# GpSimd's one-operation passes as product and addition, and VectorE's tap and copy exchanged, in the feed-forward stage of a gated cross-attention block

## The chip, the cores and the metric

The kernel runs on one core of a Trainium2 chip. Its time is the device time in microseconds (us) of one execution. The engines work side by side, each through its own instructions in order, and wait for one another by semaphores: TensorE (PE in the rows, its weight loads PEld), VectorE (DVE), ScalarE (ACT), GpSimd (POOL) and SyncE (SP), which issues the DMA transfers.

## The reference

Four batches of 1024 tokens of 512 values pass through a gated cross-attention and then through a gated feed-forward network with quantized weights and activations:

```python
def bit_linear(x, w):        # act_quant: rows scaled to 127 / max|x|, rounded; weight_quant: -1, 0, 1
    xq = x + jax.lax.stop_gradient(act_quant(x) - x)
    wq = w + jax.lax.stop_gradient(weight_quant(w) - w)
    return jnp.einsum('bsd,hd->bsh', xq, wq)
...
x = x + jnp.tanh(g_xattn[0]) * xattn(ctx, layernorm(x), mask, mask, ...)
h = bit_linear(layernorm(x), w1)                       # 512 -> 2048
h = silu(depthwise_conv1d(h, conv_w, conv_b))          # three taps along the tokens
x = x + jnp.tanh(g_ffn[0]) * bit_linear(h, w2)         # 2048 -> 512
```

## The kernel before

The program has four stages on one core: A (queries and the token part of the output), B (keys and values), C (attention) and D (feed-forward). Their instruction streams are written out by hand for each engine, and counters (the dictionaries D_DVE, D_ACT and others) tell each wait which instruction it waits for. The change lies almost wholly in stage D, the last 400 us.

**Two kinds of piece.** A *unit* n (0 to 63) is 128 of the 2048 hidden channels of one batch, over its 1024 tokens: 16 units to a batch. A *tile* m (0 to 31) is 128 tokens with all 2048 hidden channels: 8 tiles to a batch. Units have to be complete for a whole batch before its tiles can be quantized, so units of one batch are interleaved with tiles of the one before.

**A unit's way.** TensorE multiplies (`pe_first`, L1829) into one of two pairs of PSUM banks. VectorE scales the pair (`dve_scaled`, L1348). ScalarE makes the middle tap (L1111) into the buffer `h[n % 3]` and a product for the last tap (L1114). VectorE adds the remaining tap that reads PSUM (`first_tap`, L1574), after which the pair is free. GpSimd adds the last tap (`tap`, L862). TensorE turns the unit into PSUM banks 6 and 7 (`turn_units`, L1968), ScalarE applies SiLU into `hT` (L1120), and VectorE takes the largest magnitude (`biggest`, L1579).

**A tile's way.** ScalarE multiplies `hT` by the token's scale and adds MAGIC, 12582912, which rounds to integers (L1133; the first tile of a batch in two halves, L1128). GpSimd takes MAGIC off into the bf16 buffer `hi8`, which holds two tiles (`take_off`, L868; in halves L875). TensorE turns it in two parts through one bank (`turn_h`, L1958); ScalarE copies the first part out (L1139), VectorE the second (`second_half`, L1596). TensorE multiplies with the second weights (`second`, L1984), and VectorE adds the result to the residual (`add_out`, L1603), which SyncE stores.

**A step.** The loop `for m in range(-1, 32)` is written on all four engines. A step m up to 21 handles units n = 2m + 20 and n + 1, and tile m. VectorE's order in a step without extras: scale n, largest n - 3, first tap n, largest n - 2, scale n + 1, output m, copy m + 1, first tap n + 1. ScalarE's: both taps of n, SiLU n - 2, copy m + 1, rounding m + 2, both taps of n + 1, SiLU n - 1. GpSimd's: tap n, take-off m + 2, tap n + 1. Steps 22 to 31 have tiles alone. Steps 7, 15 and 23 begin with the token scales of a batch (`unit_scales`, L1583 to L1590) and the take-off in halves.

**Extras.** In steps 0 to 3 GpSimd normalizes two tiles of the last batch in each (`last_norm`, L881 and L883), and in steps 1 to 4 VectorE takes their largest magnitudes after its copy (L1198). In steps 6 to 9 GpSimd makes their integers (`last_integers`, L890 and L892). In steps 0 to 3 and 9 to 12 TensorE turns integers for the next batch (L1687) and ScalarE copies them out (L930). Ahead of the steps, units 0 to 17 run alone; there, and in step -1, a row of scales for batch 2 is made: a diagonal on VectorE (`dve_diagonal`, L1193), four matmuls (`ln_row`, L1670), a copy on ScalarE (L925).

Of the kernel before, what the change touches and what calls it, by code (L numbers as in the profile page):

```python
# [43 lines left out]
def flamingo_gated_block(nc, x, ctxT, mask, mask_cols, g_x, g_f, wsT, bk_cols, b_v, wtT, bq_cols, woT, b_out,  # L44
# [13 lines left out]
    with ExitStack() as ctx:  # L58
# [182 lines left out]
        hmax = sb("hmax", [P, KH, NT], F32)  # L241
# [220 lines left out]
        LN_DVE, _ = counts([f"{w}{i}" for i in range(NT) for w in ("stat", "aggr")] + ["rstd"] + [f"am{i}" for i in range(NT)]  # L462
# [4 lines left out]
        LN_POOL, _ = counts([f"{w}{i}" for i in range(NT) for w in ("off", "ln")] + [f"{w}{i}" for i in range(NT) for w in ("xr", "xi")])  # L467
# [359 lines left out]
        def _(pool):  # L827
# [36 lines left out]
            def take_off(m):  # L864
# [3 lines left out]
                nc.gpsimd.tensor_scalar(int_cells(m), token_cells(m), MAGIC, None, ALU.subtract).then_inc(pool_sub, 1)  # L868

            def take_off_halves(m):  # L870
                for parity, name in enumerate((f"re{m}", f"r{m}")):
# [3 lines left out]
                    nc.gpsimd.tensor_scalar(int_half(m, parity), token_half(m, parity), MAGIC, None, ALU.subtract).then_inc(pool_sub, 1)  # L875

            def last_norm(i):
                if i == 0:
                    pool.wait_ge(dve_ln, LN_DVE["rstd"])
                    pool.wait_ge(sp_xn_in, 16)  # L880
                nc.gpsimd.tensor_scalar(xn[:, i, :], xn[:, i, :], mv2[:, i, 0:1], None, ALU.subtract).then_inc(pool_ln, 1)  # L881
                pool.wait_ge(pool_ln, LN_POOL[f"off{i}"])
# [468 lines left out]
        def _(dve):  # L1351
# [229 lines left out]
            def unit_scales(b):  # L1581
# [23 lines left out]

# [470 lines left out]
```

## Time and profile before

| | us |
|---|---|
| three runs: lowest, median, highest | 1735.6, 1736.2, 1737.38 |
| the profiled execution, its own time | 1741.83 |
| its span, first to last instruction | 1739.6 |
| TensorE busy | 1601.4 (92%) |
| VectorE busy | 1109.2 (64%) |
| ScalarE busy | 833.6 (48%) |
| GpSimd busy | 933.2 (54%) |

Busy shares are means over stages with different limits. From 0 to 1340 us TensorE is busy nine tenths or more of nearly every slice; in the last 400 us it falls to eight tenths and below, and GpSimd rises to nine tenths. A wait in the trace is an engine's idle time ahead of an instruction, put down to whoever ended it. TensorE's granted clock is a share of its full 2.4 GHz; its other level is 1.2 GHz, so a mean between 0.5 and 1 is a mixture.

### The profile page before, as it was taken

The numbers are of one execution on the slowest core, as the hardware profiler recorded it, in microseconds if no ns is written. First come the engines' busy times: TensorE is split into PE (matmuls) and PEld (weight loads), VectorE is DVE, ScalarE is ACT, GpSimd is POOL, SyncE is SP. The second block draws the span as 40 slices with busy tenths as digits, with TensorE's granted clock in tenths as the row PEclk, the third lists the DMA queues.
The fourth block names the chain that finished last, engine by engine and source line by source line (L and its number), as shares of the span: only waits on it lengthen the run. The fifth ranks groups of instructions, "written<-read, shape, count | busy, mean of one in ns | idle before, by whom it ended". The sixth has DMA issues, their size and how long they took to land. (4 is left out here: it accounts for less than half of the span.)

```text
span 1739.6 us, 23634 instructions
## 1 busy us (share of the span) xinstructions
PE 1601.4 (92%) x8334; PEld 1011.1 (58%) x8370; DVE 1109.2 (64%) x2207; ACT 833.6 (48%) x972; POOL 933.2 (54%) x382
## 2 busy tenths in 40 slices
PE   6899999999999999999999999999997867898865
PEld 5788888888886544555445544554464433555532
DVE  7777636444445777767876787677269756677721
ACT  3223323333331254534573457346758765787832
POOL 1131000000000399956995699569626998998954
PEclk9899999999999999999999999999999988899988
DMA  7777557555544522313232323232351001111111
GB/s 258 254 257 259 209 176 242 194 187 187 187 164 164 194 87 75 111 49 122 87 123 97 122 95 114 86 121 78 128 172 37 19 24 37 37 49 49 50 55 49
DMA packets 116408, 217.67 MB, mean 125 GB/s; under 512 B 10056, under 2 KB 35656, under 8 KB 116304
## 3 DMA queue, kind: packets, MB, share of 16 engines
q1 hardware_dynamic: 116304, 216.31, 35.4%
q8 instruction: 62, 1.02, 0.2%
q14 instruction: 42, 0.34, 0.1%
HBM read 133.16 MB, written 83.12 MB: 124 GB/s over the span
## 5 line engine op out<-in xcount | busy, mean ns | idle before, releaser
L855 POOL TENSOR_TENSOR acc<-acc,pr 128x1024 f32<-128x1024 f32 x188 | 448.7, 2387 | 92.7 <-ACT pr L945 72.1
L945 ACT ACTIVATE pr<-ps,mcol 128x1024 f32<-128x1024 f32 x256 | 275.0, 1113 | 317.1 <-PE ps L1732 316.6
L1217 DVE CUSTOM_DVE_ANT_0 junk<-ps,mbias 128x512 bf16<-128x512 f32 x512 | 332.6, 688 | 105.6 <-PE ps L1705 105.4
L1744 PE MATMUL ps<-pr,vv 128*64 128x512 f32 x1024 | 261.1, 608 | 0.0
L836 POOL MEMSET nmt<- 128x128 f32 x1 | 0.2, 206 | 343.7 <-DVE chl L1460 343.7
L868 POOL TENSOR_SCALAR hi<-hT 128x2048 bf16<-128x2048 f32 x28 | 150.3, 5368 | 24.7 <-ACT hT L1133 20.1
L1705 PE MATMUL ps<-kh,qh 64*128 64x512 f32 x512 | 150.0, 472 | 5.7 <-DVE nmv L1217 4.9
L1705 PEld LDWEIGHTS ps<-kh,qh 64*128 64x128 f32 x512 | 68.4, 184 | 139.7 <-issue 56.4
L862 POOL TENSOR_TENSOR h_first<-h_first,last_tap 128x1023 f32<-128x1023 f32 x43 | 102.4, 2383 | 67.4 <-DVE h_first L1574 60.8
L1984 PE MATMUL ps<-w2q,hq 128*128 128x512 bf16 x505 | 128.7, 399 | 9.7 <-DVE x2t L1603 4.7
L855 POOL TENSOR_TENSOR acc<-pr 128x1024 f32<-128x1024 f32 x32 | 76.6, 2394 | 105.4 <-ACT pr L945 105.4
L1829 PE MATMUL ps<-xiT,w1q 128*128 128x512 bf16 x483 | 124.5, 402 | 5.0 <-ACT last_tap L1114 3.2
L1744 PEld LDWEIGHTS ps<-pr,vv 128*64 128x64 f32 x1024 | 60.3, 136 | 95.3 <-issue 87.2
L1958 PE MATMUL ps<-identb,hi 128*128 128x128 bf16 x512 | 44.5, 237 | 72.5 <-POOL hi L868 49.6
L1732 PE MATMUL ps<-qh,kd_hi 64*128 64x512 f32 x512 | 103.6, 397 | 0.0
L1655 PE MATMUL ps<-chh,wsh 128*128 128x512 f32 x256 | 101.5, 396 | 1.7 <-DVE chl L1460 1.7
L1732 PE MATMUL ps<-ql,kd_hi 64*128 64x512 f32 x512 | 102.5, 391 | 0.0
L1732 PE MATMUL ps<-qh,kl 64*128 64x512 f32 x512 | 102.4, 391 | 0.0
L1655 PE MATMUL ps<-wsh,chh 128*128 128x512 f32 x256 | 101.2, 395 | 0.3 <-DVE cst L1518 0.3
L1657 PE MATMUL ps<-chh,wsl 128*128 128x512 f32 x256 | 100.6, 393 | 0.0
L1656 PE MATMUL ps<-chl,wsh 128*128 128x512 f32 x256 | 100.4, 392 | 0.0
L1656 PE MATMUL ps<-wsl,chh 128*128 128x512 f32 x256 | 99.7, 389 | 0.0
(185 smaller groups left out, 3256.0 us busy)
## 6 DMA issues: line engine op xcount, KB each, us to landing
craw<-in_ctxT SPq DMA_DIRECT2D x8, 2048.0 KB, 8.7
xa<-in_x SPq DMA_DIRECT2D x32, 256.0 KB, 4.0
wraw<-in_w1T SPq DMA_DIRECT2D x16, 512.0 KB, 5.8
wraw<-in_w2T SPq DMA_DIRECT2D x16, 512.0 KB, 6.8
q_split<-kqh SPq DMA_DIRECT2D x32, 256.0 KB, 2.0
q_split<-kql SPq DMA_DIRECT2D x32, 256.0 KB, 2.3
base<-lna SPq DMA_DIRECT2D x32, 256.0 KB, 3.7
k_split<-kqh SPq DMA_DIRECT2D x32, 256.0 KB, 2.0
```

The costliest lines, as they stand in the source:

```text
L855: nc.gpsimd.tensor_tensor(acc[:, blk % 2, :], first, pr[:, (8 * blk + j) % NP, :], ALU.add).then_inc(pool_acc, 1)
L862: nc.gpsimd.tensor_tensor(units[:, 0:S - 1], units[:, 0:S - 1], last_tap[n % 2][:, 0:S - 1], ALU.add).then_inc(pool_tap, 1)
L868: nc.gpsimd.tensor_scalar(int_cells(m), token_cells(m), MAGIC, None, ALU.subtract).then_inc(pool_sub, 1)
L945: act.activation(pr[:, u % NP, :], ps[:, 2 * (u % 2):2 * (u % 2) + 2, :].rearrange("p a t -> p (a t)"), ACT.Exp, bias=mcol[:, (u // 64) * ...
L1217: dve.tensor_tensor_reduce(out=(junk1 if n < LEAD and n % 2 else junk)[:, e, :], in0=ps[:, first_bank(n) + e, :], in1=mbias[:, b % 2, kk * ...
L1655: pe.matmul(acc, lh, rh, start=k == 0, stop=False)
L1656: pe.matmul(acc, lh, rl, start=False, stop=False)
L1705: last = pe.matmul(ps[:, first_bank(n) + e, :], qh[g % 3][64 * e:64 * e + 64, i * P:(i + 1) * P], kh[g % 3][64 * e:64 * e + 64, kk * CH:(k ...
L1732: last = pe.matmul(ps[:, 2 * (u % 2) + e, :], of_keys[64 * e:64 * e + 64, :], of_tokens[64 * e:64 * e + 64, :], start=j < 2 and w == 0, st ...
L1744: last = pe.matmul(ps[64 * e:64 * e + 64, 6 + blk % 2, :], vv[g % 2][:, j, 64 * e:64 * e + 64], pr[:, u % NP, e * CH:(e + 1) * CH], start= ...
L1829: last = pe.matmul(ps[:, pair_bank(n) + t, :], w1q[:, k, j * P:(j + 1) * P], xiT[b % 2][:, k, t * 512:(t + 1) * 512], start=k == 0, stop=k ...
L1984: last = pe.matmul(ps[:, OUT_BANK, :], hq[:, m % 2, j, :], w2q[:, j, :], start=j == 0, stop=j == KH - 1)
```

## The change

On GpSimd, every pass that subtracted MAGIC becomes one that multiplies by a column of ones and adds -MAGIC: the take-off, its halves, and the second pass of `last_integers`. `last_norm` becomes one pass instead of two: times 1/std, plus -mean/std. The column -mean/std (`nmr`) is made by one small ScalarE and one small VectorE instruction while units 0 to 15 run.

On VectorE, `first_tap(n + 1)` now stands ahead of `second_half(m + 1)` in each step. The floor of 1e-5 under the token scales is a seventeenth column of `hmax`, set once, instead of an instruction (L1585) in each batch. The diagonal for batch 2 is made in round n = 14 of the first 16 units instead of in step -1, and in that round the scaling of unit 16 stands ahead of the largest of unit 12. On TensorE the row of scales for batch 2 is made in round 15, ahead of unit 17's matmuls, and unit 16's matmuls stand one round earlier, ahead of the turning of unit 12.

```diff
-        hmax = sb("hmax", [P, KH, NT], F32)
+        hmax = sb("hmax", [P, KH + 1, NT], F32)
...
-                nc.gpsimd.tensor_scalar(int_cells(m), token_cells(m), MAGIC, None, ALU.subtract).then_inc(pool_sub, 1)
+                nc.gpsimd.tensor_scalar(int_cells(m), token_cells(m), ones[:, 0:1], -MAGIC, ALU.mult, ALU.add).then_inc(pool_sub, 1)
...
-                    nc.gpsimd.tensor_scalar(int_half(m, parity), token_half(m, parity), MAGIC, None, ALU.subtract).then_inc(pool_sub, 1)
+                    nc.gpsimd.tensor_scalar(int_half(m, parity), token_half(m, parity), ones[:, 0:1], -MAGIC, ALU.mult, ALU.add).then_inc(pool_sub, 1)
...
-                nc.gpsimd.tensor_scalar(xn[:, i, :], xn[:, i, :], mv2[:, i, 0:1], None, ALU.subtract).then_inc(pool_ln, 1)
-                pool.wait_ge(pool_ln, LN_POOL[f"off{i}"])
-                nc.gpsimd.tensor_scalar(xn[:, i, :], xn[:, i, :], rs2[:, 1, i:i + 1], None, ALU.mult).then_inc(pool_ln, 1)
+                nc.gpsimd.tensor_scalar(xn[:, i, :], xn[:, i, :], rs2[:, 1, i:i + 1], nmr[:, i:i + 1],
+                                        ALU.mult, ALU.add).then_inc(pool_ln, 1)
...
-                nc.gpsimd.tensor_scalar(xi[:, i, :], xn[:, i, :], MAGIC, None, ALU.subtract).then_inc(pool_ln, 1)
+                nc.gpsimd.tensor_scalar(xi[:, i, :], xn[:, i, :], ones[:, 0:1], -MAGIC, ALU.mult, ALU.add).then_inc(pool_ln, 1)
...
-                dve.tensor_scalar(hm[:], hm[:], 1e-5, None, ALU.max).then_inc(dve_d, 1)
-                done(f"hmc{b}")
...
+            dve.memset(hmax[:, KH, :], 1e-5)
             for n in range(KH):
                 first_tap(n)
-                if n >= 2:
+                if n >= 2 and n != KH - 2:
                     biggest(n - 2)
                 dve_scaled(dve, n + 2)
+                if n == KH - 2:
+                    biggest(n - 2)
+                    dve_diagonal(dve, B - 2)
...
                     first_tap(n - 1)
-                    dve_diagonal(dve, B - 2)
...
                     add_out(m)
+                if n + 1 < UNIT_N:
+                    first_tap(n + 1)
                 if m + 1 < TILE_N:
                     second_half(m + 1)
-                if n + 1 < UNIT_N:
-                    first_tap(n + 1)
...
                 if n < KH - 3:
                     pe_first(pe, n + 3)
-                elif n == KH - 3:
+                if n == KH - 4:
                     pe_first(pe, KH)
                 elif n == KH - 1:
+                    ln_row(pe, B - 2)
                     pe_first(pe, KH + 1)
...
-                if m == -1:
-                    ln_row(pe, B - 2)
-                else:
+                if m >= 0:
                     second(m, 0)
```

Where the exchange stands on VectorE, in a step with two units (here from the scaling of unit n + 1 to the scaling of the next step's first unit). Before:

```order
L1348 TENSOR_TENSOR ps<-ps,row_148 128x1024
L1603 SCALAR_TENSOR_TENSOR x2t<-ps,hdq,x2t 128x512
L1596 COPY hq<-ps 128x1024
L1574 SCALAR_TENSOR_TENSOR h_first<-ps,convw,h_first 128x1023
L1348 TENSOR_TENSOR ps<-ps,row_148 128x1024
```

Now:

```order
L1349 TENSOR_TENSOR ps<-ps,row_148 128x1024
L1602 SCALAR_TENSOR_TENSOR x2t<-ps,hdq,x2t 128x512
L1575 SCALAR_TENSOR_TENSOR h_first<-ps,convw,h_first 128x1023
L1595 COPY hq<-ps 128x1024
L1349 TENSOR_TENSOR ps<-ps,row_148 128x1024
```

The copy stood between output and tap; it now stands between the tap and the next step's scaling.

GpSimd in a step that also normalizes two tiles. Before:

```order
L862 TENSOR_TENSOR h_first<-h_first,last_tap_140 128x1023
L868 TENSOR_SCALAR hi_149<-hT 128x2048
L862 TENSOR_TENSOR h_third<-h_third,last_tap_140 128x1023
L881 TENSOR_SCALAR xn<-xn,mv_124 128x512
L883 TENSOR_SCALAR xn<-xn,rs_125 128x512
L881 TENSOR_SCALAR xn<-xn,mv_124 128x512
L883 TENSOR_SCALAR xn<-xn,rs_125 128x512
```

Now:

```order
L863 TENSOR_TENSOR h_first<-h_first,last_tap_140 128x1023
L869 TENSOR_SCALAR hi_149<-hT,ones 128x2048
L863 TENSOR_TENSOR h_third<-h_third,last_tap_141 128x1023
L882 TENSOR_SCALAR xn<-xn,rs_125,nmr 128x512 x2
```

Four passes over 512 columns have become two, and the take-off reads the column of ones.

TensorE where the steps begin (L1968 turns a unit, L1670 is the row of scales, L1829 the first product). Before:

```order
L1829 MATMUL ps<-xiT_147,w1q 128x512 x8
L1968 MATMUL ps<-ident,h_first 128x128 x8
L1829 MATMUL ps<-xiT_147,w1q 128x512 x8
L1670 MATMUL ps<-diag,ones 128x512 x2
L1968 MATMUL ps<-ident,h_first 128x128 x8
L1829 MATMUL ps<-xiT_147,w1q 128x512 x8
```

Now:

```order
L1973 MATMUL ps<-ident,h_first 128x128 x16
L1973 MATMUL ps<-ident,h_third 128x128 x8
L1675 MATMUL ps<-diag,ones 128x512 x2
L1834 MATMUL ps<-xiT_147,w1q 128x512 x8
L1973 MATMUL ps<-ident,h_first 128x128 x8
L1834 MATMUL ps<-xiT_147,w1q 128x512 x8
```

The row of scales has moved from between units 18 and 16 to ahead of unit 17's product, behind the turning of units 12 to 14.

## Rows read from the trace of the kernel before

**Rows 1.** Windows: stretch, length, busy (count) of PE, PEld, DVE, ACT, POOL; clock, DMA.
```profile
1593.26:1603.93 10.67, 9.74 (x67) 5.85 (x67) 8.32 (x9) 9.03 (x9) 10.07 (x3) 1.00 0.15 49
1407.22:1423.62 16.40, 11.83 (x72) 6.51 (x72) 9.68 (x11) 10.16 (x9) 16.21 (x9) 0.90 0.10 33
```

**Rows 2.** Groups of POOL: names, shapes, count; busy us, mean ns; idle before.
```profile
L868 POOL TENSOR_SCALAR hi<-hT 128x2048 bf16<-128x2048 f32 x28 | 150.3, 5368 | 24.7 <-ACT hT L1133 20.1 <-PE ps L1958 4.2
L875 POOL TENSOR_SCALAR hi<-hT 128x1024 bf16<-128x1024 f32 x8 | 23.0, 2888 | 11.0 <-ACT hT L1128 11.0
L883 POOL TENSOR_SCALAR xn<-xn,rs 128x512 f32<-128x512 f32 x8 | 12.6, 1571 | 0.8
L881 POOL TENSOR_SCALAR xn<-xn,mv 128x512 f32<-128x512 f32 x8 | 12.5, 1567 | 0.0
L892 POOL TENSOR_SCALAR xi<-xn 128x512 bf16<-128x512 f32 x8 | 11.9, 1490 | 0.7
L890 POOL TENSOR_SCALAR xn<-xn,asc 128x512 f32<-128x512 f32 x8 | 5.6, 700 | 0.0
```

**Rows 3.** Timeline of step 16 into 17: start, length, engine, [idle before, ended by].
```profile
1585.89 1.22 DVE L1348 TENSOR_TENSOR ps<-ps,row 128x1024 f32<-128x1024 f32 x1
...
1587.15 1.21 ACT L1111 ACTIVATE h_first<-ps,convb,convw 128x1024 f32<-128x1024 f32 x1 [1.64 <-DVE ps L1348]
...
1589.46 1.28 DVE L1574 SCALAR_TENSOR_TENSOR h_first<-ps,convw,h_first 128x1023 f32<-128x1023 f32 x1 [1.23 <-ACT last_tap L1114]
...
1591.79 1.22 DVE L1348 TENSOR_TENSOR ps<-ps,row 128x1024 f32<-128x1024 f32 x1
...
1593.58 0.68 DVE L1596 COPY hq<-ps 128x1024 bf16<-128x1024 bf16 x1
...
1595.37 1.28 DVE L1574 SCALAR_TENSOR_TENSOR h_third<-ps,convw,h_third 128x1023 f32<-128x1023 f32 x1 [1.11 <-ACT last_tap L1114]
...
1596.57 1.22 DVE L1348 TENSOR_TENSOR ps<-ps,row 128x1024 f32<-128x1024 f32 x1
...
1598.68 0.62 PE L1958 MATMUL ps<-identb,hi 128*128 128x128 bf16 x8 [0.87 <-POOL hi L868]
```

**Rows 4.** Timeline: VectorE's scalings that open steps 0, 6, 8, 12, 21; L1198.
```profile
1367.02 1.22 DVE L1348 TENSOR_TENSOR ps<-ps,row 128x1024 f32<-128x1024 f32 x1
...
1388.49 1.27 DVE L1198 TENSOR_REDUCE floors<-xn 128x1 f32<-128x512 f32 x2
...
1455.51 1.21 DVE L1348 TENSOR_TENSOR ps<-ps,row 128x1024 f32<-128x1024 f32 x1
...
1486.72 1.23 DVE L1348 TENSOR_TENSOR ps<-ps,row 128x1024 f32<-128x1024 f32 x1 [1.52 <-PE ps L1829]
...
1538.32 1.23 DVE L1348 TENSOR_TENSOR ps<-ps,row 128x1024 f32<-128x1024 f32 x1 [0.16 <-PE ps L1829]
...
1639.29 1.22 DVE L1348 TENSOR_TENSOR ps<-ps,row 128x1024 f32<-128x1024 f32 x1
```

**Rows 5.** Timeline of step -1; L1585's durations (min/median/max in ns).
```profile
1352.94 1.22 DVE L1193 TENSOR_TENSOR diag<-ident,adq 128x1024 f32<-128x1024 f32 x1
...
1354.21 2.98 PE L1670 MATMUL ps<-diag,ones 128*128 128x512 f32 x4 [2.09 <-DVE diag L1193]
...
L1585 DVE TENSOR_SCALAR hm<-hm x4: 172/770/890, 1350.4 to 1659.7; 128x8 f32<-128x8 f32 x4
```

**Rows 6.** Timeline of the last batch's tiles, steps 23 to 29.
```profile
1660.33 2.37 ACT L1128 ACTIVATE hT<-hT,cst,hsc 128x1024 f32<-128x1024 f32 x2 [2.35 <-DVE hsc L1589]
...
1667.13 5.37 POOL L868 TENSOR_SCALAR hi<-hT 128x2048 bf16<-128x2048 f32 x1
...
1719.70 0.62 PE L1958 MATMUL ps<-identb,hi 128*128 128x128 bf16 x8 [2.73 <-POOL hi L868]
...
1721.28 2.08 ACT L1133 ACTIVATE hT<-hT,cst,hsc 128x2048 f32<-128x2048 f32 x1
...
1723.44 5.37 POOL L868 TENSOR_SCALAR hi<-hT 128x2048 bf16<-128x2048 f32 x1 [3.80 <-ACT hT L1133]
```

More of the change, by code:

```diff
@@ L461, in flamingo_gated_block @@
                                      if not (w == "r" and i == NT) and not (w == "c" and i == 0)])
-        LN_DVE, _ = counts([f"{w}{i}" for i in range(NT) for w in ("stat", "aggr")] + ["rstd"] + [f"am{i}" for i in range(NT)]
+        LN_DVE, _ = counts([f"{w}{i}" for i in range(NT) for w in ("stat", "aggr")] + ["rstd", "nmr"] + [f"am{i}" for i in range(NT)]
                            + ["amc", "rec"])
@@ L466, in flamingo_gated_block @@
         LN_LAST = {name: (B - 1) * LN_ACT_N + at for name, at in LN_LAST.items()}
-        LN_POOL, _ = counts([f"{w}{i}" for i in range(NT) for w in ("off", "ln")] + [f"{w}{i}" for i in range(NT) for w in ("xr", "xi")])
+        LN_POOL, _ = counts([f"ln{i}" for i in range(NT)] + [f"{w}{i}" for i in range(NT) for w in ("xr", "xi")])
         LN_AT = {m: ("turn", B - 2, m) for m in range(NT // 2)} | {7: ("row", B - 1, 0), 8: ("row", B - 1, 1)} \
@@ L478, in flamingo_gated_block @@
         for n in range(KH):
-            names += [f"c{n}"] + ([f"hmax{n - 2}"] if n >= 2 else []) + [f"g{n + 2}"]
+            names += [f"c{n}"] + ([f"hmax{n - 2}"] if n >= 2 and n != KH - 2 else []) + [f"g{n + 2}"]
+            names += [f"hmax{n - 2}"] if n == KH - 2 else []
         names += [f"hmax{KH - 2}", f"c{KH}"]
@@ L483, in flamingo_gated_block @@
             if m % NT == NT - 1 and m + 1 < TILE_N:
-                names += [f"hmax{n - 3}"] + [f"{w}{(m + 1) // NT}" for w in ("hm", "hmc", "hrec", "hsc", "hdq")]
+                names += [f"hmax{n - 3}"] + [f"{w}{(m + 1) // NT}" for w in ("hm", "hrec", "hsc", "hdq")]
             if m == -1:
@@ L498, in flamingo_gated_block @@
                 names.append(f"o{m}")
+            if n + 1 < UNIT_N:
+                names.append(f"c{n + 1}")
             if m + 1 < TILE_N:
                 names.append(f"hb{m + 1}")
-            if n + 1 < UNIT_N:
-                names.append(f"c{n + 1}")
         D_DVE, _ = counts(names)
@@ L918, in act_ln_std @@
             act.activation(rs2[:, 0, :], mv2[:, :, 1], ACT.Sqrt, bias=eps).then_inc(act_std2, 1)
+            act.activation(nmr[:], mv2[:, :, 0], ACT.Copy, scale=-1.0).then_inc(act_std2, 1)
         def act_ln_row(act, b):
@@ L1613, in _ @@
                     dve.reciprocal(rs2[:, 1, :], rs2[:, 0, :]).then_inc(dve_ln, 1)
+                    dve.wait_ge(act_std2, 2)
+                    dve.wait_ge(dve_ln, LN_DVE["rstd"])
+                    dve.tensor_tensor(nmr[:], nmr[:], rs2[:, 1, :], ALU.mult).then_inc(dve_ln, 1)
             biggest(KH - 2)
@@ L1635, in _ @@
                     add_out(m)
+                if n + 1 < UNIT_N:
+                    first_tap(n + 1)
                 if m + 1 < TILE_N:
                     second_half(m + 1)
-                if n + 1 < UNIT_N:
-                    first_tap(n + 1)
                 if 1 <= m < 1 + NT // 2:
```

2 lines of the change are left out of this document (1 added, 1 removed).

## The prediction

> **What bounds the kernel now.** I read the page's slices first: before stage D TensorE is full and the change touches nothing there, so only the last 400 us count. There I cut windows from one step to the next, then followed the timeline through one step of each kind. Three regimes appear.
>
> *Steps with extras (1 to 5, 7, 10, 11).* A step that normalizes two tiles takes 16.4 us and GpSimd is busy for 16.21 of it; TensorE has 11.83, at a mean clock of 0.90 [rows 1]. GpSimd sets the time.
>
> *Steps without extras (0, 8, 12, 13, 16 to 20).* A step takes 10.67 us and GpSimd is busy for 10.07 [rows 1], which looks like the same limit. The timeline says otherwise: VectorE and ScalarE hand work to and fro with no slack. Scaling of unit n at 1585.89, ScalarE's taps at 1587.15, first tap at 1589.46, a largest, scaling of n + 1 at 1591.79, first tap at 1595.37 after 1.11 us of waiting for ScalarE, scaling of the next step at 1596.57 [rows 3]. That loop closes in 1596.57 - 1585.89 = 10.68 us, and GpSimd is not in it. VectorE's output and copy (0.68) lie in the time in which it waits for ScalarE anyway.
>
> *Tiles alone (steps 23 to 31).* GpSimd's take-offs start at 1667.13 and, the seventh, at 1723.44 [rows 6]: 56.31 us for six intervals, 9.4 each. The loop is rounding 2.08, take-off 5.37, turning 0.62, ScalarE's copy, next rounding: from the end of the take-off (1719.70) to the end of the next rounding (1721.28 + 2.08) are 3.7 us, plus 5.37, is 9.1 to 9.2.
>
> **What a pass costs in the new form.** All passes of one operation are slow: 1490 ns for 512 columns and 5368 for 2048 [rows 2], so (5368 - 1490) / 1536 = 2.52 ns a column and 0.20 us fixed. One pass has product and addition with a column and a constant, L890: 700 ns for 512 columns [rows 2]. With the same 0.20 fixed this is 0.98 ns a column, and 2048 columns take 2.2 us. If nothing is fixed it is 4 x 0.70 = 2.8. Below, I take 1.9 as the end, for a fixed part of 0.28. L890 writes f32 and the take-off bf16, but L892 writes bf16 in 1490 where L881 and L883 write f32 in 1570 [rows 2], so a bf16 output has no price of its own. I take 2.2, since operations and operand kinds are L890's. Halves: 1.2 instead of 2.77 to 2.9. `last_norm`: one pass at 0.7 to 1.57 (its second scalar is a column too, which no row has), instead of two of 1.57.
>
> The Trainium skill, "GPSIMD Engine Reference", section 3.1, gives 1.03 cycles an element at 1.2 GHz for a body of at most two operations, which is 1.76 us for 2048 columns; by that the sum below would be some 3 us lower. The rule would also make the present subtraction that fast, and the trace disagrees: it takes 5.37 [rows 2].
>
> **What the exchange costs.** The copy leaves VectorE's idle time and enters the loop, between first tap n + 1 and the next scaling. VectorE is in order, so the loop grows by the copy's part, 0.63 (0.68 less the overlap seen between neighbours): 10.68 + 0.63 = 11.31 us. Who waits for the later copy: TensorE's turning of the next tile and its second half product; that turning now starts after 1598 anyway [rows 3], so nobody is late. ScalarE has 9.03 and TensorE 9.74 of work in a step [rows 1], GpSimd 4.7 + 2.2: the loop stays the bound, and the step cannot get shorter than 11.31 however fast GpSimd becomes.
>
> **The sum by stretches**, from one step's opening scaling to another's [rows 4]:
> - Units ahead of the steps, and step -1. The diagonal (1.22) and the row (2.98, waited for 2.09) leave step -1 [rows 5]. But unit 16's product now stands ahead of the turning of unit 12, and the row ahead of unit 17's product: each delays a SiLU and through ScalarE's order the taps behind it by 1 to 2 us. Walking both orders through with the row durations leaves -0.2; I take 0, bounds -2 and +2. The removed floor instruction, 172 to 890 ns [rows 5], four times, is included: some 0.2 each.
> - Steps 0 to 5: 1455.51 - 1367.02 = 88.49. After: 11.31, then four with two more VectorE passes after the copy (1.27, in the chain 1.18 [rows 4]) at 12.49, then 11.31 + 0.35 for two small reductions: 72.9. **-15.6.**
> - Steps 6 and 7: 1486.72 - 1455.51 = 31.21. The chain runs through GpSimd's integers and first half, which shrink by 2 x 0.79 + 1.55, until ScalarE's taps end later: first step +0.1, second about 12.5. **-3.8** (-1.5 to -5.5).
> - Steps 8 to 11: 51.60 becomes 4 x 11.31 = 45.2. **-6.3.**
> - Steps 12 to 15: four exchanges, +2.5, less 1.7 for the halves of step 15. **+0.8.**
> - Steps 16 to 20: 5 x 0.63. **+3.2.**
> - Step 21 to the first rounding: 1660.33 - 1639.29 = 21.04. SiLU 62 waits for a take-off that ends 3.2 us sooner, and GpSimd's last tap stands behind it. **-3.2.**
> - To the first full take-off: 6.80 becomes 4.4 (ScalarE's two halves and a rounding). **-2.4.**
> - Six intervals: 56.31. New loop 9.2 - 5.37 + 2.2 = 6.0; the first is 7.2, since TensorE's two products and two turnings stand in it. 7.2 + 5 x 6.0 = 37.2. **-19.1.**
> - The last take-off: 2.2 for 5.37. **-3.2.** What follows it is unchanged.
>
> Sum: -49.6. The span of 1739.6 becomes 1690.0. The profiled execution (1741.83) is 5.6 above the median of 1736.2; the same difference on the median gives **1686.6 us**.
>
> One more rule. When GpSimd is busy, VectorE's tiny floor instruction takes 890 ns instead of 172 [rows 5]. The Trainium skill, "SBUF — State Buffer", section "Who interferes with whom", says that a VectorE instruction using both port pairs is held until GpSimd's has ended. By that rule the wait passes to the next such instruction (the factor 127) and removing the floor saves 0.2 instead of 0.8; the sum has 0.2, and 0.8 would make it 2 us lower.
>
> **The rivals.**
> - *The exchange is free.* If the loop had slack that the rows don't show, about 20 steps lose the 0.63: -12.6, so 1674. Against it: the tap is followed by the scaling without a gap [rows 3]. 12 in 100.
> - *TensorE takes over in the tail.* Per tile it has four groups and the wait for the output's addition; should each interval be 7.2 like the first, +6; if the clock stays low there, more: 1693. 12 in 100.
> - *The pair is quick only in f32, and as slow as one operation in bf16.* Then the take-off stays 5.37, only `last_norm` halves (steps of 16.4 become 13.2, four of them, less what the first step loses: -12), and the exchange costs about +6 where GpSimd was not the bound: 1730. 5 in 100.
> - *Slower: the pair in bf16 costs two slow passes.* 2 x 5.37 - 0.2 = 10.5 a take-off. The tail's intervals become 14.3, six of them +31, the last +5; a two-unit step becomes 4.7 + 10.5 = 15.3 instead of 10.7, some 16 of them +70: about 1842. It decides from a take-off of 7 us on, where the tail's loss passes what is saved elsewhere. For it: no row has the pair with bf16. Against: L890, where the pair costs less than half of one operation. 3 in 100.
>
> **How the numbers follow.** The forecast has 68 in 100. Its own range: take-off 1.9 to 2.8 is -2 to +4.5, steps 6 and 7 about 2 either way, the start 2 either way, step lengths 0.3 on twenty: 1678 to 1697. To leave out no more than 2 in 10 it reaches into the free exchange and the slower tail: 1673 to 1701. Faster by over 0.2% (3.5 us, about what a measurement can tell from no change): 0.95; within: 0.01; slower: 0.04.
>
> **What would show it.** Right: take-offs of 2.2 us; opening scalings 11.3 us apart in steps 16 to 20, longer than 10.68 before, with the copy between tap and scaling; 12.5 in steps 1 to 4; take-offs 6.0 apart in the tail; TensorE's clock nearer 1.0 in the steps that had 0.90. Wrong: take-offs over 3 us; steps 16 to 20 at 10.7 or below; tail intervals over 7.

## The result, and the profile after

The changed kernel takes 1691.6 us (median of 4 runs, 1690.2 to 1693.4) against 1736.8 us for the kernel before in the same session (4 runs, 1735.6 to 1738.6). The ratio is 0.974, with a 95% interval from 0.9723 to 0.9756: 45 us less. The forecast was 1686.6 us, 5.0 below the measured time, and the measured time lies in the range.

First the page of the changed kernel, its span and busy times.

```profile
span 1690.2 us, 23626 instructions
...
PE 1585.7 (94%) x8334; PEld 1002.7 (59%) x8370; DVE 1104.9 (65%) x2205; ACT 830.7 (49%) x973; POOL 799.5 (47%) x374
```

GpSimd is the engine that changed. Its groups after, with count, shapes, busy us, mean ns, and the idle time before them, answer to [rows 2]:

```profile
L869 POOL TENSOR_SCALAR hi<-hT,ones 128x2048 bf16<-128x2048 f32 x28 | 55.2, 1971 | 27.8 <-ACT hT L1134 26.5
L876 POOL TENSOR_SCALAR hi<-hT,ones 128x1024 bf16<-128x1024 f32 x8 | 8.9, 1118 | 9.7 <-ACT hT L1129 9.6
L890 POOL TENSOR_SCALAR xn<-xn,asc 128x512 f32<-128x512 f32 x8 | 6.5, 813 | 0.0
L882 POOL TENSOR_SCALAR xn<-xn,rs,nmr 128x512 f32<-128x512 f32 x8 | 6.1, 770 | 0.0
L892 POOL TENSOR_SCALAR xi<-xn,ones 128x512 bf16<-128x512 f32 x8 | 5.5, 692 | 0.7
```

A take-off is 1.97 us where it was 5.37, a half 1.12 where it was 2.89, the integers 0.69 where they were 1.49, and one normalizing pass of 0.77 replaces two of 1.57. In full take-offs alone GpSimd is busy for 28 x 3.4 = 95 us less.

Now a step with two units that normalizes, and a plain one, as windows (stretch, length, busy time and count of PE, PEld, DVE, ACT, POOL, then clock, DMA share, GB/s). They answer to [rows 1].

```profile
1401.59:1414.05 12.46, 10.27 (x73) 6.21 (x73) 9.52 (x11) 9.94 (x9) 8.20 (x6) 1.00 0.13 43
1595.35:1606.62 11.27, 10.20 (x66) 5.58 (x64) 8.33 (x9) 9.03 (x8) 6.69 (x4) 1.00 0.13 47
```

The first was 16.40 us with GpSimd busy for 16.21 and a mean clock of 0.90. Now GpSimd has 8.20 of 12.46, and the clock is 1.00. The second was 10.67 and is 11.27: longer, though GpSimd's work fell from 10.07 to 6.69. The timeline of the plain step (start, length, engine, in brackets the idle time before and what ended it) shows why, against [rows 3]:

```profile
1595.35 1.22 DVE L1349 TENSOR_TENSOR ps<-ps,row 128x1024 f32<-128x1024 f32 x1
...
1598.92 1.28 DVE L1575 SCALAR_TENSOR_TENSOR h_first<-ps,convw,h_first 128x1023 f32<-128x1023 f32 x1 [1.23 <-ACT last_tap L1115]
...
1601.25 1.22 DVE L1349 TENSOR_TENSOR ps<-ps,row 128x1024 f32<-128x1024 f32 x1
...
1604.83 1.28 DVE L1575 SCALAR_TENSOR_TENSOR h_third<-ps,convw,h_third 128x1023 f32<-128x1023 f32 x1 [1.71 <-ACT last_tap L1115]
...
1606.03 0.68 DVE L1595 COPY hq<-ps 128x1024 bf16<-128x1024 bf16 x1
...
1606.62 1.23 DVE L1349 TENSOR_TENSOR ps<-ps,row 128x1024 f32<-128x1024 f32 x1
```

VectorE's wait ahead of the step's second tap grew from 1.11 to 1.71 us, because the copy no longer fills it. The copy now stands behind the tap, and the next scaling behind the copy. The step is 0.60 us longer.

Last, the tiles alone, as windows over seven take-offs (from the start of the first to the end of the last), before and then after:

```profile
1667.00:1728.81 61.81, 38.53 (x212) 19.27 (x216) 8.78 (x13) 19.05 (x13) 37.69 (x8) 0.85 0.14 47
```

```profile
1640.29:1679.69 39.40, 31.57 (x204) 16.21 (x208) 8.78 (x13) 18.89 (x13) 13.80 (x7) 0.96 0.22 74
```

GpSimd's 37.7 us of work became 13.8, the stretch lost 22.4, and the granted clock went from 0.85 to 0.96. Within it, after:

```profile
1640.29 1.97 POOL L869 TENSOR_SCALAR hi<-hT,ones 128x2048 bf16<-128x2048 f32 x1 [0.87 <-ACT hT L1134]
...
1648.81 1.97 POOL L869 TENSOR_SCALAR hi<-hT,ones 128x2048 bf16<-128x2048 f32 x1 [6.56 <-ACT hT L1134]
...
1671.94 1.97 POOL L869 TENSOR_SCALAR hi<-hT,ones 128x2048 bf16<-128x2048 f32 x1 [3.81 <-ACT hT L1134]
...
1675.55 2.08 ACT L1134 ACTIVATE hT<-hT,cst,hsc 128x2048 f32<-128x2048 f32 x1
...
1677.72 1.97 POOL L869 TENSOR_SCALAR hi<-hT,ones 128x2048 bf16<-128x2048 f32 x1 [3.81 <-ACT hT L1134]
...
1679.75 0.62 PE L1963 MATMUL ps<-identb,hi 128*128 128x128 bf16 x8 [0.54 <-POOL hi L869]
...
1680.41 1.02 ACT L1140 ACTIVATE hq<-ps 128x1024 bf16<-128x1024 bf16 x1 [2.78 <-PE ps L1963]
```

The take-offs at 1671.94 and 1677.72 are 5.78 us apart (9.4 before, [rows 6]). GpSimd now waits 3.81 us in each interval for ScalarE's rounding. The loop is the same, with a shorter take-off in it.

### The profile page after: what moved, and what is told of

Read it like the earlier page. It is cut to its first block and busy times, and to the rows that moved or that the text cites. A ratio compares the mean times of both kernels' runs of the same rounds, so it can differ in the third digit from the quotient of the medians.

```text
span 1690.2 us, 23626 instructions
## 1 busy us (share of the span) xinstructions
PE 1585.7 (94%) x8334; PEld 1002.7 (59%) x8370; DVE 1104.9 (65%) x2205; ACT 830.7 (49%) x973; POOL 799.5 (47%) x374
## 5 line engine op out<-in xcount | busy, mean ns | idle before, releaser
L1710 PEld LDWEIGHTS ps<-kh,qh 64*128 64x128 f32 x512 | 68.5, 184 | 139.4 <-issue 56.4
L1989 PE MATMUL ps<-w2q,hq 128*128 128x512 bf16 x505 | 121.3, 382 | 16.8 <-ACT xiT L931 9.2
L1834 PE MATMUL ps<-xiT,w1q 128*128 128x512 bf16 x483 | 116.6, 382 | 7.2 <-DVE h_first L1575 3.2
L1662 PE MATMUL ps<-wsh,chl 128*128 128x512 f32 x256 | 99.8, 390 | 0.0
L1989 PEld LDWEIGHTS ps<-w2q,hq 128*128 128x128 bf16 x512 | 48.3, 98 | 78.2 <-issue 20.9
```

Source lines behind the costliest of these rows:

```text
L1662: last = pe.matmul(acc, ll, rh, start=False, stop=k == n - 1)
L1710: last = pe.matmul(ps[:, first_bank(n) + e, :], qh[g % 3][64 * e:64 * e + 64, i * P:(i + 1) * P], kh[g % 3][64 * e:64 * e + 64, kk * CH:(k ...
L1834: last = pe.matmul(ps[:, pair_bank(n) + t, :], w1q[:, k, j * P:(j + 1) * P], xiT[b % 2][:, k, t * 512:(t + 1) * 512], start=k == 0, stop=k ...
L1989: last = pe.matmul(ps[:, OUT_BANK, :], hq[:, m % 2, j, :], w2q[:, j, :], start=j == 0, stop=j == KH - 1)
```

## The experiments

Single profiled executions are compared below by stage D alone, from the scaling of unit 14 to the end of the span: 407.2 us before, 361.1 after. The code ahead of it computes the same in all kernels, yet in the twelve traces of this case that scaling starts anywhere from 1326.2 to 1332.4 us; the two ends are `b_exchange` and the kernel before, whose instructions ahead of it are the same ones. The table gives where the time lies in stage D, read to 0.1 us. "Opening" is from unit 14's scaling to step 0, "rest" from step 21's opening scaling to the end. The opening is the least certain column: `after` and `diag_first` have the same code there and differ by 1.1 us.

| kernel | median us | stage D | opening | steps 0-5 | 6-7 | 8-11 | 12-15 | 16-20 | rest |
|---|---|---|---|---|---|---|---|---|---|
| before | 1736.8 | 407.2 | 34.6 | 88.5 | 31.2 | 51.6 | 47.6 | 53.4 | 100.3 |
| after | 1691.6 | 361.1 | 36.3 | 72.7 | 30.1 | 45.1 | 48.2 | 56.4 | 72.3 |
| c_forms | 1681.8 | 350.0 | 34.6 | 69.2 | 28.5 | 43.1 | 48.0 | 53.4 | 73.2 |
| b_exchange | 1744.3 | 413.7 | 35.2 | 88.6 | 30.8 | 52.3 | 49.2 | 56.4 | 101.2 |
| a_old_start | 1692.9 | 361.0 | 34.8 | 72.7 | 30.9 | 45.1 | 48.7 | 56.4 | 72.4 |
| a_copy_first | 1680.9 | 349.5 | 35.7 | 69.2 | 27.7 | 43.1 | 47.6 | 53.4 | 72.9 |
| e_slow | 1721.8 | 393.7 | 36.9 | 72.7 | 29.3 | 49.6 | 48.9 | 56.4 | 100.0 |
| forms | one run | 377.4 | 36.2 | 72.7 | 30.1 | 45.1 | 48.2 | 56.4 | 88.7 |
| v_b | 1679.7 | 351.2 | 34.7 | 71.8 | 26.8 | 44.2 | 47.2 | 53.5 | 73.1 |
| v_br | 1735.9 | 404.8 | 35.8 | 81.7 | 30.8 | 49.6 | 56.5 | 67.0 | 83.3 |
| diag_first | one run | 359.0 | 35.2 | 72.7 | 28.9 | 45.1 | 48.2 | 56.4 | 72.6 |
| copy_first_old_start | 1678.4 | 346.6 | 34.0 | 69.3 | 26.6 | 43.1 | 47.2 | 53.4 | 73.0 |

The first question was which of the three parts of the change brought what. The prediction's theory is that the forms bring all of it, the exchange costs 0.6 us wherever VectorE's loop is the bound, and the new start brings nothing. Its rival is that the exchange is free, or pays by making GpSimd's last tap earlier.

### a_copy_first: the change without the exchange

```diff
-                if n + 1 < UNIT_N:
-                    first_tap(n + 1)
...
+                if n + 1 < UNIT_N:
+                    first_tap(n + 1)
```

`second_half(m + 1)` lies between the two places, so the copy comes first again.

> The changed kernel with VectorE's copy ahead of the tap again. Theory (the loop between VectorE and ScalarE sets the steps with two units, and the exchange put the copy's 0.6 us into it): opening scalings 10.7 us apart instead of 11.27 in steps 16 to 20, 11.9 instead of 12.46 in steps 1 to 4, some 0.6 us on each of 22 steps, and 1.8 us more in step 6, where the diagonal stands behind the copy: -14 us, about 1677. Rival (with the quick take-off another engine sets the step, TensorE with its 9.7 us of work or a tap that waits for a copy that waits for TensorE): steps stay at 11.2 or more, within 3 us of 1691.

Measured: 1680.9 us (1677.6 to 1683.4), ratio to before 0.9663 (0.9646 to 0.968): 10.8 us faster than the change by the medians, 11.6 less in stage D. The expected 14 was too much: steps 12 to 15 gain 0.6 in all, and the rest is 0.6 longer. Its plain step as a window and as VectorE's timeline (two consecutive plain steps):

```profile
1594.00:1604.67 10.67, 9.84 (x64) 5.62 (x64) 8.33 (x9) 9.02 (x9) 6.69 (x4) 1.00 0.16 51
```

```profile
1592.94 1.22 DVE L1349 TENSOR_TENSOR ps<-ps,row 128x1024 f32<-128x1024 f32 x1
...
1594.73 0.68 DVE L1595 COPY hq<-ps 128x1024 bf16<-128x1024 bf16 x1
...
1596.52 1.28 DVE L1575 SCALAR_TENSOR_TENSOR h_third<-ps,convw,h_third 128x1023 f32<-128x1023 f32 x1 [1.11 <-ACT last_tap L1115]
...
1597.72 1.22 DVE L1349 TENSOR_TENSOR ps<-ps,row 128x1024 f32<-128x1024 f32 x1
...
1608.39 1.22 DVE L1349 TENSOR_TENSOR ps<-ps,row 128x1024 f32<-128x1024 f32 x1
```

The copy is in front, the wait for ScalarE is 1.11 again, the scaling follows the tap, and the step is 10.67. In both kernels GpSimd has 6.69 us of work in it. So the loop between VectorE and ScalarE is the bound, and the exchange lengthened it (`v_b` below shows how much of that loop is ScalarE's own work). Steps 1 to 4 are 11.9 instead of 12.46, as expected.

### b_exchange: the kernel before, with the exchange alone

```diff
-                if m + 1 < TILE_N:
-                    second_half(m + 1)
...
+                if m + 1 < TILE_N:
+                    second_half(m + 1)
```

> The kernel before with the exchange of tap and copy alone. Theory: where the loop sets the step (0, 8, 12, 13, 16 to 20) it grows by 0.6 us, where GpSimd sets it nothing changes; +5 to +8 us, about 1743. Rival (the exchange serves a GpSimd that waits for the tap): GpSimd's second tap starts sooner and the steps with extras shorten: -1 to -5 us.

Measured: 1744.3 us (1742.1 to 1745.9), ratio 1.0036 (1.0023 to 1.0048): 6.5 us slower than its own before. Steps 16 to 20 are 11.27 long (+3.0 in all), steps 0 to 5 together as long as before (88.6 for 88.5). Of these, steps 0 and 1 grew by 0.6 and 0.5, and steps 2 to 5, where GpSimd was the bound, gave it back (65.8 to 64.8). Once GpSimd is quick, the same exchange costs 3.5 us in those steps, which is most of the difference between 6.5 here and 11.6 above. In neither kernel does the exchange pay in sum; the rival's gain of 1 to 5 us did not come.

### c_forms: the kernel before, with the new passes alone

```diff
-                nc.gpsimd.tensor_scalar(int_cells(m), token_cells(m), MAGIC, None, ALU.subtract).then_inc(pool_sub, 1)
+                nc.gpsimd.tensor_scalar(int_cells(m), token_cells(m), ones[:, 0:1], -MAGIC, ALU.mult, ALU.add).then_inc(pool_sub, 1)
```

with the same in the halves and in `last_integers`, and `last_norm` as one pass.

> The kernel before with the new forms of GpSimd's passes alone (take-off, halves, integers, one normalizing pass with its column); order of all engines, floor instruction and start as before. Theory: all of the gain and more, since the rest costs: 45 + 14 + 1 us below before, about 1676 to 1678. Rival (part of the gain needs the reordering): no lower than 1688.

Measured: 1681.8 us (1679.5 to 1683.4), ratio 0.9678 (0.9661 to 0.9694). Stage D loses 57.2 us. The whole change loses 46.1, so the forms bring more than all of the gain, though not quite as much as expected (1676 to 1678).

### a_old_start: the change with the diagonal, the row and the product where they stood

```diff
-                if n == KH - 2:
-                    biggest(n - 2)
-                    dve_diagonal(dve, B - 2)
...
+                    dve_diagonal(dve, B - 2)
...
-                if n == KH - 4:
+                elif n == KH - 3:
...
-                    ln_row(pe, B - 2)
...
-                if m >= 0:
+                if m == -1:
+                    ln_row(pe, B - 2)
+                else:
```

> The changed kernel with the diagonal, the row of scales and unit 16's product where they were before. Theory from the two traces (from the scaling of unit 14 to that of unit 20 took 36.3 us after and 34.6 before): 1.7 us less, about 1690. Rival (the earlier diagonal is what keeps the start short now that GpSimd's halves are quick): 1 to 3 us more.

Measured: 1692.9 us (1690.8 to 1694.4), ratio 0.9735 (0.9718 to 0.9751), not to be told from the change's 0.974. Stage D is 361.0 against 361.1. Neither the expected 1.7 us less nor the rival's loss is seen. The opening is 1.5 us shorter, and steps 6 to 15 give 1.3 of that back.

### e_slow: the change with the take-offs and halves as one subtraction again

The edit is that of `c_forms` backwards, for `take_off` and its halves only. It comes near the third rival, in which the pair is slow with bf16; in that rival the integers (L892), which are bf16 too, would be slow as well.

> The changed kernel with the take-off and its halves as a subtraction again (5.37 us); integers, the single normalizing pass, the exchange and the start stay changed. Theory (the take-off carries nearly all of the gain): the tail's intervals are 9.2 to 9.4 us again, steps with extras are GpSimd's again at some 13 us, the others 11.3: what is left is the normalizing passes less the exchange, 3 to 9 us below before, about 1731. Rival (the shorter normalizing and integer passes carry a good part): 15 us or more below before.

Measured: 1721.8 us (1719.3 to 1726.8), ratio 0.9905 (0.9876 to 0.9934). Its take-offs:

```profile
L869 POOL TENSOR_SCALAR hi<-hT 128x2048 bf16<-128x2048 f32 x28 | 150.2, 5364 | 25.1 <-ACT hT L1134 24.4
```

The expected 1731 was wrong, and the other theory on record (15 us or more below before) came close: with 5.36 us a take-off this kernel is still 14.8 us faster than before. The steps that normalize are 12.46 long, exactly as with the quick take-off, not the 13.2 of the prediction's third rival. I had given the normalizing pass its slow end there, 1.57; it takes 0.77. Those 2 x 0.8 us less put GpSimd's work in such a step at 11.58 us, below the loop's 12.46:

```profile
1401.38:1413.84 12.46, 10.28 (x73) 6.22 (x73) 9.52 (x12) 9.94 (x9) 11.58 (x6) 1.00 0.14 43
```

So the quick take-off is worth 30 us by the medians (1721.8 - 1691.6). Of the 32.6 in stage D, 27.7 lie in the rest, where tiles run alone, and 4.5 in steps 8 to 11.

### forms: what makes the pass quick

In the change's kernel the take-off of tile m takes one of six forms by m % 6 (each branch is put on one line here):

```diff
+    if m % 6 == 1:   done_ = ins(out_, in_, ones[:, 0:1], -MAGIC, ALU.mult, ALU.add)
+    elif m % 6 == 2: done_ = ins(out_, in_, 1.0, -MAGIC, ALU.mult, ALU.add)
+    elif m % 6 == 3: done_ = ins(out_, in_, -MAGIC, None, ALU.add)
+    elif m % 6 == 4: done_ = ins(out_, in_, MAGIC, 1.0, ALU.subtract, ALU.mult)
+    elif m % 6 == 5: done_ = ins(out_, in_, -MAGIC, 1.0, ALU.add, ALU.mult)
+    else:            done_ = ins(out_, in_, MAGIC, None, ALU.subtract)
```

> The changed kernel with the full take-off of tile m in one of six forms by m modulo 6, each on a line of its own: subtraction of MAGIC; times the column of ones, plus -MAGIC; times the constant 1, plus -MAGIC; plus -MAGIC alone; minus MAGIC, times 1; plus -MAGIC, times 1. Theory (GpSimd has a quick way for product then addition and a slow one for all else): 1.97 us for the two forms of product then addition, 5.4 for the single operations, 5.4 or more for the two other pairs. Rival (two operations, whichever they are, take the quick way): 1.97 for four forms. Second rival (addition is quick and subtraction slow): 1.97 for all forms with an addition.

Measured, as groups of GpSimd, in the order of the diff (lines 872, 874, 876, 878, 880, 882):

```profile
L872 POOL TENSOR_SCALAR hi<-hT,ones 128x2048 bf16<-128x2048 f32 x6 | 11.9, 1978 | 5.3 <-ACT hT L1148 5.1
```

```profile
L874 POOL TENSOR_SCALAR hi<-hT 128x2048 bf16<-128x2048 f32 x4 | 7.6, 1900 | 7.6 <-ACT hT L1148 7.4
```

```profile
L876 POOL TENSOR_SCALAR hi<-hT 128x2048 bf16<-128x2048 f32 x5 | 26.9, 5375 | 4.0 <-ACT hT L1148 3.8
```

```profile
L878 POOL TENSOR_SCALAR hi<-hT 128x2048 bf16<-128x2048 f32 x4 | 28.4, 7099 | 4.3 <-ACT hT L1148 4.2
```

```profile
L880 POOL TENSOR_SCALAR hi<-hT 128x2048 bf16<-128x2048 f32 x5 | 9.5, 1900 | 4.2 <-ACT hT L1148 4.2
```

```profile
L882 POOL TENSOR_SCALAR hi<-hT 128x2048 bf16<-128x2048 f32 x4 | 21.5, 5370 | 5.0 <-ACT hT L1148 4.9
```

The column of ones plays no part: with the constant 1.0 the pass is even 0.08 us quicker. Nor does the order: addition then product takes the same 1.90 as product then addition. A single addition is as slow as a single subtraction (5.37). The one pair tried with a subtraction, subtraction then product, is the slowest, 7.10; product then subtraction was not tried. A single product, by a column, was slow too: 1.57 us for 512 columns (L883, [rows 2]). Quick is the pair of product and addition, and of the forms tried nothing else. None of the three theories on record had that: addition before product was expected to be slow by the first, a single addition to be quick by the last, and all four pairs to be quick by the second.

### v_b: the largest behind the copy

With the copy in front, `biggest(n - 2)` moved behind `second_half`, so that VectorE's wait for ScalarE is spent on it too.

```diff
-                if n - 2 < UNIT_N:
+                if n - 2 < UNIT_N <= n + 1:
                     biggest(n - 2)
...
+                if n + 1 < UNIT_N:
+                    biggest(n - 2)
```

> As a_copy_first (copy ahead of the tap), and VectorE's largest of unit n - 2 moved from ahead of the scaling of unit n + 1 to behind the copy, into the time in which VectorE waits for ScalarE's taps. Theory (between the taps of n and those of n + 1 ScalarE's own work takes the same 5.89 us as VectorE's chain): steps stay at 10.67, time as a_copy_first. Rival (VectorE's chain alone holds that half of the step): 1.1 us less on each step, 9.7 to 10.0, down to TensorE's work, 12 to 20 us less.

Measured: 1679.7 us (1678.3 to 1682.8), ratio 0.9663 (0.9641 to 0.9686), the same as `a_copy_first`. Plain steps stay at 10.68. A plain step, timeline of VectorE and ScalarE:

```profile
1589.23 1.22 DVE L1351 TENSOR_TENSOR ps<-ps,row 128x1024 f32<-128x1024 f32 x1
...
1589.63 2.11 ACT L1136 ACTIVATE hT<-hT,cst,hsc 128x2048 f32<-128x2048 f32 x1
...
1591.61 1.22 ACT L1114 ACTIVATE h_third<-ps,convb,convw 128x1024 f32<-128x1024 f32 x1
```

VectorE's scaling of unit n + 1 now comes 1.20 us after its first tap (2.32 in `a_copy_first`) and ends at 1590.45. But ScalarE goes through its copy and the rounding (2.11) first and begins the taps at 1591.61, without a gap. So in this half of the step ScalarE's own work takes as long as VectorE's chain did, as the theory on record says, and shortening VectorE's chain alone gains nothing. Steps 9 to 13, most of them with turned integers, are 11.15 instead of 10.7 to 10.85. Step 1 is 14.47 instead of 11.97; its second scaling waits 2.47 us for TensorE's product, and why the product is late there was not followed up. Steps 6 and 7, 0.9 us shorter together, don't make up for it in stage D.

### v_br: the rounding and the take-off later

As `v_b`, and in steps with two units ScalarE's rounding of tile m + 2 behind its last SiLU, and GpSimd's take-off behind its last tap.

```diff
+                if not last and m + 2 < TILE_N and (m + 2) % NT and late:
+                    round_up(m + 2)
...
+                if m + 2 < TILE_N and (m + 2) % NT and late:
+                    take_off(m + 2)
```

> As v_b, and ScalarE's rounding of tile m + 2 moved behind the second SiLU of the step, with GpSimd's take-off behind its second tap. Theory: the first half of the loop falls to 4.8 us and the second rises to 5.3, so 10.1 to 10.2 us a step instead of 10.67: 8 to 12 us less than a_copy_first, about 1670, if the take-off, now ready 2.5 us later against the next step, doesn't come too late for the SiLU that overwrites its tile. Rival (it comes too late, or TensorE, with 9.7 us of work, loses its order): 10.7 us or more a step.

Measured: 1735.9 us (10 runs, 1732.0 to 1737.7), ratio 0.999 (0.9976 to 1.0005). The rival was right, and the whole gain is gone. One late step, timeline:

```profile
1611.30 1.98 POOL L874 TENSOR_SCALAR hi<-hT,ones 128x2048 bf16<-128x2048 f32 x1
...
1613.33 0.75 PE L1976 MATMUL ps<-identb,hi 128*128 128x128 bf16 x8 [3.16 <-POOL hi L874]
...
1613.87 3.49 PE L1847 MATMUL ps<-xiT,w1q 128*128 128x512 bf16 x8
...
1617.40 1.23 DVE L1360 TENSOR_TENSOR ps<-ps,row 128x1024 f32<-128x1024 f32 x1 [3.74 <-PE ps L1847]
```

The take-off ends at 1613.28 (1611.30 + 1.98). TensorE's turning waits 3.16 us for it, and the next unit's product stands in the queue behind the turning. VectorE then waits 3.74 for that product, which itself takes 3.49 us where it takes 1.89 in a plain step of `a_copy_first`: after the wait TensorE's clock is low for a while (a mean of 0.88 over the step, 1.00 there). Steps 16 to 20, of 10.68 each in `v_b`, became 10.7 to 14.6 long.

### diag_first and copy_first_old_start: steps 6 and 7, and the start once more

After these runs steps 6 and 7 were the largest term still unexplained. In step 6 of the changed kernel VectorE and GpSimd do this:

```profile
1448.74 0.68 DVE L1595 COPY hq<-ps 128x1024 bf16<-128x1024 bf16 x1
...
1449.34 2.99 DVE L1194 TENSOR_TENSOR diag<-ident,adq 128x1024 f32<-128x1024 f32 x1
```

```profile
1448.90 2.35 POOL L863 TENSOR_TENSOR h_first<-h_first,last_tap 128x1023 f32<-128x1023 f32 x1 [3.54 <-DVE h_first L1575]
1451.23 1.66 POOL L890 TENSOR_SCALAR xn<-xn,asc 128x512 f32<-128x512 f32 x1
```

The diagonal takes 2.99 us instead of the 1.22 of [rows 5]. Between tap and diagonal now stands the copy. By its end GpSimd's tap has begun (1448.90), and the diagonal, which reads two tiles of SBUF, starts behind it. `diag_first` puts the diagonal ahead of the copy in step 6:

```diff
+                if m == 6:
+                    dve_diagonal(dve, B - 1)
...
-                if m == 6:
-                    dve_diagonal(dve, B - 1)
```

> The changed kernel with the diagonal of step 6 ahead of the copy instead of behind it. Theory (in the changed kernel the copy lets GpSimd's tap start first, and the diagonal, with two inputs in SBUF, is held until the tap ends: 2.99 us instead of 1.22): the diagonal takes 1.2 to 1.4 us again, the tap some 0.9 us more, and step 6 falls from 16.3 to about 14.7. Rival (it waits for something else, or the two slow each other in any order): step 6 within 0.5 of 16.3.

Measured, one run: 1688.3 us, stage D 359.0, 2.1 less than after; 1.1 of that lies in the opening, where the code is the same, and 1.2 in steps 6 and 7. In step 6:

```profile
1445.69 1.22 DVE L1194 TENSOR_TENSOR diag<-ident,adq 128x1024 f32<-128x1024 f32 x1
```

```profile
1445.85 3.27 POOL L863 TENSOR_TENSOR h_first<-h_first,last_tap 128x1023 f32<-128x1023 f32 x1 [3.54 <-DVE h_first L1575]
```

Now the diagonal takes 1.22, and GpSimd's tap pays 0.9 us for it (3.27). In the other order GpSimd did not get off free: its next pass, L890 at 1451.23, ran beside the delayed diagonal and took 1.66 us, where all the others of that line take 0.69. Step 6 falls from 16.31 to 14.82. The Trainium skill, "SBUF — State Buffer", section "Who interferes with whom", says that the engine whose instruction was issued first decides who is blocked. By that rule order alone should move the wait from one engine to the other, and the two traces agree: 2.99 and 2.35 in one order, 1.22 and 3.27 in the other. The kernel before had the better order, with 1.22 and 3.27 too. With the quick passes GpSimd has room for 0.9 us (7.91 us of work in a step of 14.82), and VectorE's loop has none for 1.8.

`copy_first_old_start` is `a_copy_first` together with `a_old_start`; it asks whether the new start is worth anything without the exchange.

> The changed kernel with the copy ahead of the tap, and the start of the steps as it was before: the candidate for the fastest. From the stretches of a_copy_first and c_forms: 348.5 to 349.5 us from the scaling of unit 14 to the end, against 361.1 of the changed kernel and 349.5 of a_copy_first: about 1680, level with a_copy_first. Rival (the earlier diagonal pays with the copy first): 1 to 2 us above a_copy_first.

Measured: 1678.4 us (1676.1 to 1679.3), ratio 0.9659 (0.9642 to 0.9676), the quickest of all here: 13.2 us below the change, 58.6 below its own before. Its stage D is 2.9 us shorter than that of `a_copy_first`, of which 1.7 lie in the opening and 1.1 in steps 6 and 7. The medians show 2.4, with ranges that overlap, and they come from two sessions whose own kernel before stood at 1737.8 and 1737.1. The five kernels with the old start open in 34.0 to 35.2 us, the seven with the new one in 34.7 to 36.9. That the old start is better is therefore likely, not shown.

## Why the prediction was right, and where it was not

**The bound of each regime held.** Steps with extras were bound by GpSimd, but for step 1, which the prediction counts among those of 16.4 us and which was 11.97 long and grew with the exchange (12.46 in `b_exchange`). With quick passes those that normalize are as long as VectorE's loop, 12.46 (predicted 12.49). Plain steps were bound by the loop and not by GpSimd's 10.07 of work: `b_exchange` made them 0.60 longer with the slow passes, `a_copy_first` left them at 10.67 with the quick ones. Tiles alone went with the take-off. One thing the loop's account left out: the half of it in which VectorE waits for ScalarE holds as much of ScalarE's own work (`v_b`).

**The take-off.** Predicted 2.2 with ends of 1.9 and 2.8, from L890 alone; it is 1.97. The 2.2 took the fixed part of a single operation, 0.20; the two sizes in the new form (0.692 and 1.971) give 0.27. The lower end, for a fixed part of 0.28, works out to 1.96 and not 1.9. The rival of two slow passes was out, by the row that the prediction held against it, L890. But the price has nothing to do with bf16, in which that rival saw the danger. What matters is which two operations are paired: subtraction then product costs 7.10 us, just beyond the 7 us from which the prediction had its slower case. The gain hangs on the pair being a product and an addition.

**The terms, in stage D** (predicted; measured): steps 0 to 5 (-15.6; -15.8), steps 8 to 11 (-6.3; -6.5), steps 12 to 15 (+0.8; +0.6), steps 16 to 20 (+3.2; +3.0), step 21 to the first full take-off (-5.6; -5.45), six intervals (-19.1; -18.9: 37.43 us for a predicted 37.2, the first longer at 8.52 for 7.2, the others shorter at 5.78 for 6.0), the last take-off and the end (-3.2; -3.7). Each is right to 0.5 us, that of the six intervals by luck: the first was 1.3 too short and the other five together 1.1 too long. Two are not, or not as near:

- *Steps 6 and 7: -3.8 predicted, with bounds of -1.5 and -5.5; -1.1 measured.* This step failed, and the bounds with it. Step 6 was to grow by 0.1 and grew by 1.5 (14.82 to 16.31). The prediction walked the chain with the diagonal at 1.22 us and did not ask what GpSimd does at that moment once the copy stands in between; `diag_first` shows that as the cause, since it brings step 6 back to 14.82. Step 7 was to take about 12.5 and took 13.83. Its chain does reach the last scaling at 12.3, but the scaling then waits 1.49 us for TensorE's product. The prediction had only walked VectorE, ScalarE and GpSimd, although the same scaling waited 1.52 us for the same product in the kernel before ([rows 4], 1486.72). From the trace after:

```profile
1462.73 1.04 PE L1963 MATMUL ps<-identb,hi 128*128 128x128 bf16 x8 [0.86 <-ACT hq L1140]
1463.56 2.02 PE L1680 MATMUL ps<-diag,ones 128*128 128x512 f32 x2
1465.80 2.41 PE L1834 MATMUL ps<-xiT,w1q 128*128 128x512 bf16 x7 [0.22 <-issue]
```

```profile
1468.24 1.23 DVE L1349 TENSOR_TENSOR ps<-ps,row 128x1024 f32<-128x1024 f32 x1 [1.49 <-PE ps L1834]
```

  The product stands behind the row of scales (2.02), and the row behind a turning that waited for ScalarE's copy. TensorE's granted clock in this step is low as well, 0.63 (0.69 before). That this makes the product late is read from the trace and not tested; `diag_first` leaves step 7 at 14.06. The window of step 7 after, in the columns used above:

```profile
1454.41:1468.24 13.83, 8.27 (x34) 4.91 (x36) 7.29 (x8) 11.80 (x11) 9.25 (x6) 0.63 0.11 39
```

- *The start: 0 predicted, with bounds of 2; +1.7 measured.* Within the bounds. `a_old_start` (34.8 for 36.3) points at the moved instructions, but does not show it: `diag_first` has the same code there and opened in 35.2, at a granted clock of 0.90 where the trace after has 0.86. The openings of the two, after and then `diag_first`:

```profile
1329.08:1365.40 36.32, 24.22 (x119) 14.06 (x120) 25.39 (x26) 25.73 (x25) 20.12 (x11) 0.86 0.00 1
```

```profile
1327.16:1362.32 35.16, 23.09 (x119) 13.64 (x120) 25.41 (x27) 25.76 (x25) 20.17 (x11) 0.90 0.00 1
```

  So of the 1.7, as much as 1.1 can be the trace and not the change.

**Span and median.** The span was forecast at 1690.0 and is 1690.2, which looks better than it is. Stage D lost 46.1 and not 49.6. The missing 3.5 are offset by stage D beginning 3.3 us earlier in the second trace (1329.1 for 1332.4), with the same work ahead of it. The median was missed by 5.0, since the prediction took the 5.6 us between the profiled execution of before and the median as a constant. Of the kernel after, the profiled execution lies 0.7 above its median. So the last step of the sum failed: of the 4.9 between 5.6 and 0.7, 3.3 were the late stage D in that one execution, and 1.6 stay unexplained. The change of stage D, put on the median instead, gives 1736.2 - 49.6 = 1686.6 by the prediction's sum, and 1736.2 - 46.1 = 1690.1 with the measured terms, 1.5 from the measured 1691.6.

**The rivals.** *The exchange is free* is refuted: it costs 11.6 us of stage D in the changed kernel, and undoing it is what the change left on the table. *TensorE takes over in the tail* did not come, but for the first interval of 8.52: the others are 5.78, and the clock rose to 0.96. *The pair slow in bf16* would have given some 1722 (`e_slow`, with its integers quick) or a little more, not 1730.

**The floor instruction.** In [rows 5] it took 0.77 us in the median and 0.89 at most. It is gone, and the factor 127 behind it now takes up to 0.63 (0.40 before), by the view of its durations, least, median and most in ns, after:

```profile
L1588 DVE TENSOR_SCALAR hsc<-hsc x4: 172/190/627, 1351.4 to 1635.6; 128x8 f32<-128x8 f32 x4
```

The 0.63 is that of the first batch, and it ends at 1351.98, as GpSimd's tap ends at 1351.95. There the wait passed on, as by the rule of the Trainium skill, "SBUF — State Buffer", section "Who interferes with whom", that the prediction draws on. In the other three batches the factor takes 0.21 at most, so most of the wait did not pass on. Four floors are too small a term to be seen in the sum.

## What to carry to other kernels

Where a quick engine's pass comes down, look first at which loop closes next, and keep everything out of it: an exchange that cost 6.5 us while GpSimd was the bound of many steps cost 11.6 us of the 57.2 that the quick passes had won. When instructions of VectorE move against GpSimd's, ask for each what GpSimd runs at that moment and which of the two can afford the wait. And take a change's worth from stretches between fixed points of the trace, not from whole spans, for the offset of a profiled execution to the median is no constant.

## What was not expected of the hardware

- GpSimd's pass over 128x2048, f32 to bf16, takes 1.90 us as a pair of product and addition in either order (1.97 with a column of ones), 5.37 as one addition or one subtraction, and 7.10 as subtraction and product. Less arithmetic is slower, by 2.8 times.
- A constant in the place of the column of ones saves 0.08 us a pass.
- Of the diagonal on VectorE and the tap on GpSimd, the one that begins second pays: VectorE 1.8 us (2.99 for 1.22), or GpSimd 0.9 (3.27 for 2.35).
- With the same code ahead of it, stage D begins up to 6.2 us apart from one profiled execution to another (1326.2 us in `b_exchange`, 1332.4 in the kernel before).
- With the same code, the opening of stage D took 36.32 us in one execution and 35.16 in another.
